# A macaron block on one core: softmax shares taken on GpSimd before the value product, head outputs produced transposed, inverse roots by logarithm and one Newton step

## What is computed

```python
x = x + 0.5 * F(layernorm(x))
x = x + attention(layernorm(x))          # softmax over 1024 keys, one head
x = x + 0.5 * F(layernorm(x))
```

```python
h = shift_token(x)
q, k, v = split(h @ wqkv)
q = l2norm(q) * qs                       # divide by the root of the sum of squares
k = l2norm(k) * ksc
q, k = rotary_xpos(q, k)
sim = where(mask, -big, einsum('bhwid,bhwjd->bhwij', 8 * q, k))   # own window and the one before
o = einsum('bhwij,bhwjd->bhwid', softmax(sim), v)
x = x + o @ wo
h = layernorm(shift_token(x)) @ w1 + b1
a, g = split(h)
x = x + (a * gelu(g)) @ w2 + b2
```

## Time and profile before

| | us |
|---|---|
| median of 3 runs | 3174.26 (3171.78 to 3177.37) |
| the profiled execution, its time | 3177.26 |
| its span, first to last instruction | 3175.5 |
| PE busy | 3081.3 (97%) |
| DVE busy | 2697.3 (85%) |
| ACT busy | 2268.3 (71%) |
| POOL busy | 1674.1 (53%) |

### The profile page before, as it was taken

The page is one execution under the profiler, slowest core; times in us unless marked ns, Lnnn a source line. Parts: engine busy times, 40 slices in busy tenths (PEclk is TensorE's granted clock), DMA queues, the critical chain, the costliest instruction groups (busy, mean ns, idle before and its releaser), DMA issues.

```text
span 3175.5 us, 83658 instructions
## 1 busy us (share of the span) xinstructions
PE 3081.3 (97%) x30466; PEld 2208.4 (70%) x30497; DVE 2697.3 (85%) x6053; ACT 2268.3 (71%) x5488; POOL 1674.1 (53%) x1000
## 2 busy tenths in 40 slices
PE   6999999999999999989999699999999999999999
PEld 3777777666777777657777477777766677777765
DVE  6999999678999888768999599999966889899865
ACT  4888888537888888328888388888853688888842
POOL 6788776215666565441000578878621466666610
PEclk9999999999999999999999799999999999999999
DMA  4111112201111112200000011111211111111211
GB/s 115 32 34 34 32 36 44 51 20 31 32 35 33 32 39 46 48 9 1 1 1 1 18 34 36 32 32 32 50 48 21 31 32 36 32 32 40 48 38 50
DMA packets 136852, 107.18 MB, mean 34 GB/s; under 512 B 80937, under 2 KB 102402, under 8 KB 136450
## 3 DMA queue, kind: packets, MB, share of 16 engines
q1 hardware_dynamic: 136450, 101.83, 14.2%
HBM read 12.67 MB, written 4.19 MB: 5 GB/s over the span
## 4 chain that ended last, share of the span: by engine, by line
PE 92%; DVE 4%; issue 2%; ACT 1%; DMA 0%; SPq 0%; DVEq 0%; ACTq 0%
PE psum L1172 15%; PE psum L1044 10%; PE psum L1149 7%; PE psum L1194 7%; PE psum L1216 7%; PE psum L1183 7%; PE psum L1101 7%; PE psum L1070 5%; PE psum L1135 4%; PE psum L1230 3%; PE psum L1243 3%; PE psum L1416 3%; PE psum L1392 3%; PE psum L1089 2%; PE psum L1125 2%
## 5 line engine op out<-in xcount | busy, mean ns | idle before, releaser
L421 POOL TENSOR_TENSOR rnorm<-ssq_floor,neg_half 128x16 f32<-128x16 f32 x256 | 746.3, 2915 | 725.3 <-DVE qkr L739 691.8
L426 POOL TENSOR_TENSOR qk_cos<-qk_cos,qk_sin 128x1024 f32<-128x1024 f32 x256 | 606.3, 2368 | 0.0
L496 ACT ACTIVATE shared<-psum,neg_max 128x128 f32<-128x128 f32 x2048 | 582.5, 377 | 27.1 <-DVE neg_max L715 27.0
L1172 PE MATMUL psum<-wqkv,hT 128*128 128x512 f32 x1024 | 558.0, 629 | 22.2 <-DVE qk_sin L700 9.7
L503 ACT ACTIVATE sq<-psum 128x512 f32<-128x512 f32 x512 | 318.2, 621 | 115.5 <-PE psum L1172 115.4
L700 DVE TENSOR_TENSOR qk_sin<-psum,sin 128x256 f32<-128x256 f32 x1024 | 381.7, 414 | 22.2 <-ACT sq L503 21.4
L556 ACT ACTIVATE shared<-psum,b1g 128x512 f32<-128x512 f32 (+1 forms) x192 | 131.2, 685 | 353.5 <-PE psum L1044 349.3
L706 DVE TENSOR_TENSOR qk_cos<-psum,cos 128x512 f32<-128x512 f32 x512 | 348.1, 681 | 13.5 <-ACT sq L503 13.3
L531 ACT COPY shared<-psum 128x512 f32<-128x512 f32 x512 | 276.4, 592 | 111.1 <-PE psum L1216 111.0
L715 DVE TENSOR_REDUCE neg_max<-psum 128x4 f32<-128x512 f32 x512 | 327.7, 682 | 31.5 <-PE psum L1103 29.7
L1044 PE MATMUL psum<-shared,w1g 128*128 128x512 f32 (+1 forms) x768 | 347.4, 596 | 7.2 <-DVE shared L805 5.3
(11 more groups left out here) (134 smaller groups left out, 6468.2 us busy)
## 6 DMA issues: line engine op xcount, KB each, us to landing
vprev<-v SPq DMA_DIRECT2D x512, 130.0 KB, 2.3
shared<-Y SPq DMA_DIRECT2D x32, 256.0 KB
shared<-Y SPq DMA_DIRECT2D x32, 254.0 KB
X<-in_L_attn_x SPq DMA_DIRECT2D x8, 512.0 KB, 6.9
out<-X SPq DMA_DIRECT2D x8, 512.0 KB, 3.5
wqkv<-in_L_ffn_wqkv SPq DMA_DIRECT2D x4, 768.0 KB, 4.4
w<-in_L_ffn_w SPq DMA_DIRECT2D x4, 341.0 KB
wo<-in_L_ffn_wo SPq DMA_DIRECT2D x4, 256.0 KB, 5.2
```

The lines of the kernel that those rows point to most:

```text
L421: nc.gpsimd.tensor_tensor(rnorm[:], ssq_floor[:], neg_half[:], ALU.pow).then_inc(rnorm_ready, 1)
L426: nc.gpsimd.tensor_tensor(both, both, qk_sin[:, t.m % 2, :], ALU.add).then_inc(sum_ready, 1)
L496: last = nc.scalar.activation(probs[:, c * P:(c + 1) * P], bank(3 + i, (c % 4) * P, (c % 4 + 1) * P), ACT.Exp, bias=neg_max[:, c:c + 1])
L1172: nc.tensor.matmul(bank(i), hT[:, t.m * P:(t.m + 1) * P], wqkv[:, i * INNER:(i + 1) * INNER], start=True, stop=True).then_inc(qk_psum, 1)
```

## The change

The change rewrites how the local attention is divided among the engines.

- The softmax division moves ahead of the value product. DVE sums the exponentials straight from SBUF (`sums`, two reductions of 128x512) and inverts eight sums a row (`inverse_sums`); POOL multiplies the exponentials with them in two halves (`shares`). `probs` gets a second buffer.
- The value product swaps its operands: the values are the loaded operand and the transposed probabilities move, so that the heads' outputs arrive transposed in bank 5. `heads_transpose` and the column of ones are gone.
- From tile 4 of each layer on, the inverse root is no longer a power on POOL: ACT takes the logarithm and an exponential of minus half of it (`rough_root`), and POOL does one Newton step in four small instructions (`refine`). Sums of squares are scaled by 256 squared, to lie in the range of the logarithm. ACT loads a table that holds both functions at slot 0 of each layer. The floor is now a `tensor_tensor` against the constant tile `least` (L763 before).
- Probabilities of tile s-1, no longer of tile s, are transposed in slot s; values are projected for tile s+2 and tokens transposed for tile s+5. PSUM banks are dealt anew.

The core of the diff:

```diff
-HD1 = DH + 1
+NORM_SCALE = 256.0
...
-        ssq_floor = sb("ssq_floor", [P, 16])
-        rnorm = sb("rnorm", [P, 16])
+        ssq_floor = sb("ssq_floor", [P, 2, 16])
+        least = sb("least", [P, 16])
+        log_ssq = sb("log_ssq", [P, 16])
+        rough = sb("rough", [P, 2, 16])
+        step = sb("step", [P, 3, 16])
+        rnorm = sb("rnorm", [P, 2, 16])
...
+        probs = [shared[:, 7 * N:8 * N], shared[:, 9 * N:10 * N]]
...
-            return 0 if t.L and t.row < 3 else 5
+            return 0 if t.L and t.row < 2 else 7
...
+            def refine(t):
+
+                i, r = refined(t), rough[:, t.m % 2, :]
+                pool.wait_ge(rough_ready, i + 1)
+                nc.gpsimd.tensor_tensor(step[:, 0, :], r, r, ALU.mult).then_inc(step_ready, 1)
+                pool.wait_ge(step_ready, 3 * i + 1)
+                nc.gpsimd.tensor_tensor(step[:, 1, :], step[:, 0, :], ssq_floor[:, t.m % 2, :],
+                                        ALU.mult).then_inc(step_ready, 1)
+                pool.wait_ge(step_ready, 3 * i + 2)
+                nc.gpsimd.tensor_scalar(step[:, 2, :], step[:, 1, :], -0.5, 1.5, ALU.mult,
+                                        ALU.add).then_inc(step_ready, 1)
+                pool.wait_ge(step_ready, 3 * i + 3)
+                wait(pool, qkr_ready, before(t, 2))
+                nc.gpsimd.tensor_tensor(rnorm[:, t.m % 2, :], r, step[:, 2, :], ALU.mult).then_inc(rnorm_ready, 1)
...
+            def shares(t):
+                wait(pool, rsum_ready, before(t, 0))
+                for i in range(2):
+                    part = probs[t.m % 2][:, i * BANK:(i + 1) * BANK].rearrange("p (h k) -> p h k", k=P)
+                    nc.gpsimd.tensor_tensor(part, part, rsum[:, 4 * i:4 * i + 4].unsqueeze(2).to_broadcast([P, 4, P]),
+                                            ALU.mult).then_inc(share_ready, 1)
...
-                if t := tile_at(L, s + 4):
+                if s < 0 and (t := tile_at(L, s + 4)):
                     root(t)
                     total(t)
+                if s >= 1 and (t := tile_at(L, s + 3)):
+                    total(t)
+                    refine(t)
+                if t := tile_at(L, s):
+                    shares(t)
...
-                wait(act, probsT_psum, before(t, 1, 2))
+                wait(act, probsT_psum, before(t, 2, 2))
...
+            def rough_root(t):
+
+                i = refined(t)
+                wait(act, floor_ready, before(t, 0))
+                nc.scalar.activation(log_ssq[:], ssq_floor[:, t.m % 2, :], ACT.Ln).then_inc(log_ready, 1)
+                act.wait_ge(log_ready, i + 1)
+                wait(act, rnorm_ready, before(t, 2))
+                nc.scalar.activation(rough[:, t.m % 2, :], log_ssq[:], ACT.Exp, scale=-0.5).then_inc(rough_ready, 1)
...
-                wait(act, oT_psum, before(t, 0))
+                wait(act, pv_ready, before(t, 0))
...
+                if s == 0:
+                    nc.scalar.preload_act_table_set("natural_log_exp_and_others")
+                if s <= 0 and (t := tile_at(L, s + 4)):
+                    tokens(t)
+                if s >= 0 and (t := tile_at(L, s + 2)):
+                    values(t)
                 if t := tile_at(L, s + 4):
-                    tokens(t)
-                if t := tile_at(L, s - 2):
-                    outputs(t)
+                    squares(t, 0)
+                if t := tile_at(L, s):
+                    exponents(t, 0)
+                    exponents(t, 1)
                 if s == NT:
                     gated(group_at(L, 0), 0)
                     gated(group_at(L, 0), 1)
+                if t := tile_at(L, s - 1):
+                    weights(t)
+                if s >= 0 and (t := tile_at(L, s + 5)):
+                    tokens(t)
+                if t := tile_at(L, s + 4):
+                    squares(t, 1)
+                if s < 0 and (t := tile_at(L, s + 2)):
+                    values(t)
+                if t := tile_at(L, s + 2):
+                    rotated(t)
+                if t := tile_at(L, s - 1):
+                    outputs(t)
+                if s >= 1 and (t := tile_at(L, s + 3)):
+                    rough_root(t)
...
+                for i in range(2):
+                    part = probs[t.m % 2][:, i * BANK:(i + 1) * BANK].rearrange("p (h k) -> p h k", k=P)
+                    dve.wait_ge(probs_ready, 2 * t.n + i + 1)
+                    nc.vector.tensor_reduce(total_probs[:, 4 * i:4 * i + 4], part, AX_X, ALU.add).then_inc(total_ready, 1)
+
+            def inverse_sums(t):
+                dve.wait_ge(total_ready, 2 * t.n + 2)
+                wait(dve, share_ready, before(t, 1, 2))
+                nc.vector.reciprocal(rsum[:], total_probs[:]).then_inc(rsum_ready, 1)
...
-                nc.vector.tensor_scalar_max(ssq_floor[:], ssq[:], 1e-24).then_inc(floor_ready, 1)
+                wait(dve, rnorm_ready, before(t, 2))
+                nc.vector.tensor_tensor(ssq_floor[:, t.m % 2, :], ssq[:], least[:], ALU.max).then_inc(floor_ready, 1)
...
-                if t := tile_at(L, s - 1):
-                    sums(t)
                 if s == NT - 2:
                     centre(group_at(L, 0))
                 if t := tile_at(L, s + 2):
                     norms(t)
-                if t := tile_at(L, s - 1):
-                    shares(t)
                 if t := tile_at(L, s + 4):
                     queries(t)
-                if t := tile_at(L, s - 2):
+                if t := tile_at(L, s):
+                    sums(t)
+                if s <= NT and (t := tile_at(L, s - 2)):
                     add_heads(t)
+                if t := tile_at(L, s):
+                    inverse_sums(t)
...
+                if x_bank(t) == 6 and t.row < 6:
                     wait(pe, hT_ready, before(t, 1, 2))
+                    if t.L == DEPTH and t.row == 5:
+                        pe.wait_ge(g_o, NT)
+                    elif t.row == 5:
+                        wait(pe, y_ready, NG * t.L)
                 elif x_bank(t) == 6:
-                    wait(pe, probsT_ready, 2 * (t.n - 5) + 1)
+                    wait(pe, probsT_ready, 2 * (t.n - 6) + 1)
...
-            def heads_transpose(t):
-
-                wait(pe, o_ready, before(t, 0, 2))
-                if u := tile_at(t.L, t.row + 4):
-                    wait(pe, v_ready, before(u, 0))
-                else:
-                    wait(pe, oT_ready, before(t, 1))
-                for c in range(INNER // P):
-                    last = nc.tensor.transpose(bank(5, c * P, (c + 1) * P), o[:, c * P:(c + 1) * P], ident[:])
-                last.then_inc(oT_psum, 1)
-
             def weigh_values(t):
 
                 pe.wait_ge(vprev_ready[t.m % 4], 32 * (t.n // 4 + 1))
-                if u := tile_at(t.L, t.row + 2):
-                    wait(pe, qT_ready, before(u, 0))
-                wait(pe, o_ready, before(t, 1, 2))
+                wait(pe, oT_ready, before(t, 1))
                 pe.wait_ge(probsT_ready, 2 * t.n + 2)
-                for h in range(HEADS):
-                    at_h = (h % 2) * BANK + (h // 2) * P
-                    col = (h % 4) * HD1
-                    bk = (7, 2)[h // 4]
-                    nc.tensor.matmul(bank(bk, col, col + HD1, slice(WIN, P)),
-                                     probsT[:, at_h + WIN:at_h + P], v[:, t.m % 4, h, :],
-                                     start=True, stop=True)
-                    last = nc.tensor.matmul(bank(bk, col, col + HD1, slice(0, WIN)),
-                                            probsT[:, at_h:at_h + WIN], vprev[:, t.m % 4, h, :],
-                                            start=True, stop=True)
+                for hh in range(HEADS // 2):
+                    for w, keys in enumerate((vprev, v)):
+                        for i in range(2):
+                            at = i * BANK + hh * P + w * WIN
+                            last = nc.tensor.matmul(bank(5, hh * P + w * WIN, hh * P + (w + 1) * WIN,
+                                                         slice(DH * i, DH * i + DH)),
+                                                    keys[:, t.m % 4, 2 * hh + i, :], probsT[:, at:at + WIN],
+                                                    start=True, stop=True)
                 last.then_inc(pv_ready, 1)
...
-                pe.wait_ge(probs_ready, 2 * t.n + i + 1)
+                pe.wait_ge(share_ready, 2 * t.n + i + 1)
...
+                elif s < NT:
+                    if s == 0:
+                        tokens_transpose(tile(4))
+                        if L % DEPTH:
+                            combine(group_at(L - 1, NG - 1))
+                        if L == 0:
+                            pe.wait_ge(consts_done, 10)
+                    if t := tile(2):
+                        project_v(t)
+                    scores(tile(0))
+                    if t := tile(4):
+                        project_qk(t, 0)
+                        project_qk(t, 1)
```

(46 more changed lines are left out.)

169 lines of the change are left out of this document (71 added, 98 removed).

## The result

The changed kernel takes 3526.2 us (median of 4 runs, 3511.4 to 3530.3), the kernel before 3174.0 beside it: 1.11 times as long, with an interval of 1.107 to 1.113. Two executions that ran at a lower granted clock are left out of all numbers here: one of experiment 11 (3505.5 us at 0.845) and one of the kernel before (3925.8 us at 0.75). I had said 3372, with 3235 to 3450: right in direction, short by 154 us, and outside the range.

What follows compares the result with a forecast made beforehand. PE bound the kernel at 8.55 us a slot; ring B with the ports, 8.41 + 0.95 = 9.36, would take over. 232 x (9.36 - 8.55) = 188, plus 10, from 3177.3 gives 3375, as median 3372; range 3235 to 3450.

Steps and rivals of the forecast that it cites:

- PE's slot of 8.55 before, and that a ring would take over: Local attention: PE's instructions set 8.55 us a slot before; the new order makes PE wait in a ring.
- Its own work, forecast at 8.12: PE's instructions per slot: four transposes of heads' outputs go, 8.55 - 0.43 = 8.12 us.
- DVE stays under that: DVE's work per slot stays under 8.83 us, as reciprocals, shares and the floor's excess go and two reductions come.
- ring A: PE and ACT: tokens' transposes wait in bank 6 for ACT's first copy of transposed probabilities; 8.83 us a slot.
- The sign that I had named for it: PE idle 0.7 at L1178, released by L577, with a slot of 8.8, if the ports were wrong.
- Ring D: Not named in the prediction: maxima, `norms`, queries' products, keys' transposes waiting for bank 0, value product, value projection, scores.
- The second reckoning of the ports: Should POOL keep the ports for both halves of `shares`, DVE runs 1.19 later; the slot comes to 9.35 us.
- Ring B, 8.41: Through POOL: `refine`, shares, PE's transposes, ACT's copies and rough root, back to `refine`; 8.41 us, 9.36 with the ports.
- the rival of dear POOL instructions: POOL's small instructions cost 0.5 each, ring B grows by 0.6 on top of the ports: 3511 us; chance 0.06.
- The ports, 0.95 on ring B: `norms` on DVE and `shares` on POOL block each other at the shared SBUF ports, adding 0.95 us a slot.
- the first rival: The ports don't matter for `norms`, so ring A bounds: 3249 us; chance 0.21.
- The narrower range: Range of the forecast case, 3330 to 3440 us, from 0.1 less and 0.3 more for `refine`, root and ports.

Runs made afterwards that it cites:

- experiment 11: Kernel of experiment 10 with PE transposing queries ahead of keys and DVE adding the heads right behind `norms`: 3209.3 us, 1.0116 times before.
- experiment 12: Kernel of experiment 11 with DVE adding the heads between the sine and cosine products of the queries: 3171.5 us, 0.9989 times before.
- experiment 3: Changed kernel with POOL making the shares before `refine` instead of after it: 3524.0 us, 1.110 times before.
- experiment 4: Changed kernel with heads added before the sums and shares made before `refine`: 3393.7 us, 1.069 times before.
- experiment 5: Kernel of experiment 4 with PE making the tokens' transposes last in a slot: 3364.5 us, 1.060 times before.
- experiment 7: Changed kernel with the sums of the exponentials written by ACT's accumulator instead of DVE: 3493.5 us, 1.100 times before.
- experiment 2: Changed kernel with PE making the tokens' transposes last in a slot, behind the value product: 3523.8 us, 1.110 times before.
- experiment 10: Kernel of experiment 5 with one more wait: POOL starts `total` only after DVE's `norms` of the slot: 3234.3 us, 1.0185 times before.
- experiment 9: Changed kernel with POOL's power of 16 columns back in place of `refine` and ACT's rough root: 3472.9 us, 1.093 times before.

## Why the prediction was wrong

- **PE's slot of 8.55 before, and that a ring would take over.** Right. PE fell to 88%, within the 85 to 90% that I named. Its own work, forecast at 8.12, is about 8.2 by experiment 12.
- **The step that failed: "DVE stays under that".** I added up DVE's instructions against 8.83 and never followed what stands behind what. The sum was fair, since DVE is 80% busy. But on DVE `add_heads` stands behind maxima, `norms`, queries' products and the new sums, and PE's bank 2 waits for `add_heads`: ring C, 9.92. It could have been summed as the others were. By my own terms it is an estimate of 9.4 before any collision: maxima 1.27, `norms` 1.1, queries' products 1.4, two sums of 0.6, the heads 0.3, and 4.1 for PE (its 4.5 less the keys' transposes). That is above ring A's 8.83; 9.56 was measured (experiment 3), and 9.92 with the collision. Moving `add_heads` alone gives back 177 us, more than the 154 by which I was short.
- **Ring A, 8.83.** The ring exists and is 9.06 where it binds (experiments 4, 5 and 7): 0.10 too little for the projection and ACT's reaction (308.87 to 310.03, 1.16 instead of 1.06) and 0.15 too little for copy and wake-up (0.79 from 312.52 to 313.31, instead of 0.64). PE's part, 4.65, measured 4.61 (310.27 to 314.88 in experiment 4). In the changed kernel it isn't the bound, though it shows 0.69 of idle time. The sign that I had named for it, PE idle 0.7 at L1178 released by L577, appeared (0.69), and experiment 2 shows that it meant nothing for the time.
- **Ring D, in passing.** The second reckoning of the ports (maxima, wait, `norms`, sines and cosine, PE's 4.5) walked a ring through DVE. It stops at the cosine product, so it is ring D and not ring C. Its terms add up to 8.27, and with the wait of 1.19 to 9.46, not to 9.35; without a collision ring D measured 8.74 (experiment 10).
- **Ring B, 8.41.** The bound in no run: PE hardly ever waits for the shares. Shares were 2.04 instead of 2.45, `refine` 1.07 instead of 1.40 (307.60 to the shares at 308.67), logarithm and exponential 0.22 each for 0.20. So the rival of dear POOL instructions, 3511 and the nearest number to the result, didn't happen.
- **The ports, 0.95 on ring B.** The mechanism is right, and against the first rival: experiments 3, 5, 9 and 10 show it. The size is 0.36 in the changed kernel, and it stands in ring C. I had `norms` asked for in the first half of `shares`; it came in the last 0.5 of the second half, since the shares started 0.6 earlier against the maxima than by my phases. In experiment 5 it is 0.95, the number forecast, but for another pair, `total` and `norms`: a coincidence. L786 at 1.57 is just under the 1.6 to 2.0 that I named.
- **The skill's rule.** The Trainium skill (SBUF — State Buffer, "Who interferes with whom") has the shared ports held for the whole instruction against the other engine. The runs agree in both orders, for two SBUF inputs: `norms` behind the shares 1.57, behind `total` 2.17, and POOL's one-column add behind `norms` 1.08 instead of 0.24. In two places they don't. The power of experiment 9 reads SBUF too and runs beside the whole of `norms`, and neither is held (2.91 and 1.24). And in experiment 4 POOL's product of 128 columns starts 0.11 ahead of `norms`, by the records, and is yet the one that is held.
- **The range.** 3235 to 3450 held rings A and B with and without the ports, and nothing for a ring that I had not seen. No rival stood for one more ring. The narrower range, "0.1 less and 0.3 more", is 3349 to 3442 by its own terms, not 3330 to 3440.

## What to carry to other kernels

After a change of order, sum rings and not engines: for each wait of the engine that bound before, walk back through what stands ahead of the releaser on its own engine until you are back at the start, and do it for every bank that is shared. An idle piece in the trace is no price; the one that binds is found by cutting it, and the same edit that is worth nothing today may be worth 0.3 us a slot once the longer ring is gone. When DVE reads two SBUF tensors, see what POOL reads at that moment in every kind of slot: a wait that keeps them apart can be cheaper than none.

## What the runs showed of the hardware

- A POOL instruction that reads 1024 columns makes DVE's two-input product of 1024 columns, 1.22 us alone, last 2.17 (experiment 5) or 2.22 (experiment 4) where they overlap most. A power of 16 columns on POOL, 2.91 us long, leaves it at 1.24. So it is not POOL being busy that costs; that it is the amount read fits, but no run varies it alone.
- It works on instructions with one tensor input on POOL too: the subtraction and product of 128 columns, 0.81 alone, took 1.85 beside `norms` (experiment 4, 307.06 to 308.91), while `norms` took 1.23. DVE's sums, 1.27 with one SBUF input, were as long beside `total` as without; the floor of the kernel before, one SBUF input as well, was held (161 ns alone, median 544).
- ACT's accumulator costs a reading instruction of 0.20 to 0.25 us for each exponential of 128 columns, 0.09 of which lengthens the row.
- POOL's operations of 16 columns take 0.20 to 0.22 us and follow each other, each waiting for the last, in 0.30. Its product of 512 columns with a broadcast factor takes 1.04.
